# A windowed-attention decoder on one core: scores on alternating row halves, one sine product, VectorE's step reordered

## What is computed

```python
for i in range(DEPTH):                       # 6
    x = attn_layer(shift_tokens(x), Wqkv[i], q_scale[i], k_scale[i], Wo[i]) + x
    x = ffn_layer(shift_tokens(x), ln_g[i], ln_b[i], W1[i], b1[i], W2[i], b2[i]) + x

def attn_layer(x, Wqkv, qs, ksc, Wo):
    q, k, v = (sh(t) for t in jnp.split(x @ Wqkv, 3, -1))      # 16 heads of 64
    q, k = l2norm(q) * qs, l2norm(k) * ksc
    q = q * cos * scale + rotate_half(q) * sin * scale
    k = k * cos * inv + rotate_half(k) * sin * inv
    sim = q @ k.T * QK_SCALE                                   # a key is seen 0 to 32 tokens back
    return softmax(where(mask, -max, sim)) @ v @ Wo            # heads merged before Wo
```

## Time and profile before

| | |
|---|---|
| median of 3 runs | 4648.19 us (4643.84 to 4649.11) |
| the profiled execution | 4650.33 us, span 4648.5 us |
| TensorE matmul / VectorE / ScalarE / GpSimd busy | 93% / 83% / 78% / 73% of the span |
| mean granted clock of TensorE | 0.969 |
| a layer, from one L1460 of VectorE to the next | 658.6 us, of it 542.7 us from the first to the last L1352 (128 of them) |

### The profile page before, as it was taken

One profiled execution on the slowest core, in us unless ns is written; L12 is line 12 of the kernel. 1 busy time (PEld: TensorE's weight loads), 2 busy tenths in 40 slices (PEclk: granted clock), 3 DMA queues, 4 the chain that ended last, 5 costly groups with the idle time before them and its releaser, 6 DMA issues.

```text
span 4648.5 us, 135499 instructions
## 1 busy us (share of the span) xinstructions
PE 4341.6 (93%) x47296; PEld 3494.1 (75%) x47296; DVE 3854.4 (83%) x9773; ACT 3635.1 (78%) x11591; POOL 3383.3 (73%) x2447
## 2 busy tenths in 40 slices
PE   7988869999889999889999799998899998899997
PEld 5666647888768888678888678887688886788886
DVE  7988878888778888778888688887788887788886
ACT  6889967888748888658888478887488886588884
POOL 4544448888658888568888388886588885688882
PEclk9999989999989999989999999999899999899998
DMA  2000000000000000000000000000000000000000
GB/s 76 0 0 1 0 14 2 0 0 0 6 20 1 0 0 0 6 20 0 0 0 1 24 2 0 0 0 6 19 1 0 0 0 6 6 0 0 0 1 19
DMA packets 31380, 26.63 MB, mean 6 GB/s; under 512 B 10308, under 2 KB 23490, under 8 KB 31170
## 3 DMA queue, kind: packets, MB, share of 16 engines
q1 hardware_dynamic: 31170, 23.96, 1.8%
HBM read 21.85 MB, written 2.10 MB: 5 GB/s over the span
## 4 chain that ended last, share of the span: by engine, by line
PE 75%; DVE 12%; issue 7%; ACT 3%; POOL 2%; DVEq 0%; SPq 0%; DMA 0%; ACTq 0%; POOLq 0%
PE bank L659 17%; PE bank L706 13%; PE bank L754 10%; PE bank L732 9%; PE bank L652 7%; PE bank L717 7%; PE bank L820 4%; PE bank L692 4%; DVE top L1270 3%; PE bank L834 2%; DVE qk_parts L1245 2%; PE bank L635 1%; DVE qk_t L1406 1%; DVE by_sin L1238 1%; ACT prob L888 1%
## 5 line engine op out<-in xcount | busy, mean ns | idle before, releaser
L1070 POOL TENSOR_TENSOR rotated<-by_cos,by_sin 128x512 f32<-128x512 f32 x768 | 981.4, 1278 | 394.6 <-DVE by_sin L1320 377.3
L1078 POOL TENSOR_TENSOR rnorm<-norm2g,neg_half 128x16 f32<-128x16 f32 x384 | 1115.5, 2905 | 163.7 <-DVE norm2g L1333 163.7
L963 ACT ACTIVATE bank<-bank,top 128x128 f32<-128x128 f32 x3072 | 1064.1, 352 | 10.9 <-DVE top L1340 4.0
L1090 POOL TENSOR_TENSOR rotated<-rotated,rnorm 128x512 f32<-128x512 f32 x768 | 786.5, 1047 | 0.5
L1312 DVE TENSOR_TENSOR by_cos<-bank,rot_cos 128x512 f32<-128x512 f32 x768 | 531.2, 692 | 256.9 <-PE bank L659 248.6
L945 ACT ACTIVATE qk_t<-bank 128x512 f32<-128x512 f32 x768 | 459.9, 599 | 286.5 <-PE bank L652 285.9
L706 PEld LDWEIGHTS bank<-qk_t 64*64 64x64 f32 x12288 | 529.2, 133 | 193.0 <-issue 193.0
L706 PE MATMUL bank<-qk_t 64*64 64x64 f32 (+1 forms) x12288 | 674.2, 237 | 0.0
L963 ACT ACTIVATION_READ_ACCUMULATOR bank<-bank,top 128x1 f32 x3072 | 669.4, 218 | 0.0
L659 PE MATMUL bank<-wqkv_high,xt_high 128*128 128x512 f32 (+1 forms) x1536 | 598.6, 390 | 11.0 <-ACT vout L974 11.0
L1320 DVE TENSOR_TENSOR by_sin<-bank,rot_sin 128x256 f32<-128x256 f32 x1536 | 572.9, 415 | 0.0
(11 more groups left out here) (148 smaller groups left out, 8904.1 us busy)
## 6 DMA issues: line engine op xcount, KB each, us to landing
wqkv_sb<-in_L_ffn_Wqkv_dram SPq DMA_DIRECT2D x36, 256.0 KB, 4.1
wo_sb<-in_L_ffn_Wo_dram SPq DMA_DIRECT2D x48, 64.0 KB, 2.0
out_dram<-y SPq DMA_DIRECT2D x8, 256.0 KB, 3.5
w_sb<-in_L_ffn_W_dram SPq DMA_DIRECT2D x6, 341.0 KB, 3.0
w_sb<-in_L_ffn_W_dram SPq DMA_DIRECT2D x12, 64.0 KB
cst<-in_constants_dram SPq DMA_DIRECT2D x1, 518.0 KB, 3.5
b_sb<-in_L_ffn_b_dram SPq DMA_DIRECT2D x1, 384.0 KB
w_sb<-in_L_ffn_W_dram SPq DMA_DIRECT2D x6, 42.5 KB
```

The costliest lines, as they stand in the source:

```text
L963: last = nc.scalar.activation(at, at, ACT.Exp, bias=top[jl % 2][:, h:h + 1], accum_out=psum_raw[jl % 2][:, h:h + 1])
L1070: nc.gpsimd.tensor_tensor(rotated[j % 4][:, :, :, :], by_cos[j % 2][:, :, :, :], by_sin[j % 2][:, :, :, :], ALU.add).then_inc(c_rot, 1)
L1078: nc.gpsimd.tensor_tensor(rnorm[slot][:, :, :].rearrange("t g n -> t (g n)"), norm2g[slot][:, :, :].rearrange("t g n -> t (g n)"), neg_hal ...
L1090: nc.gpsimd.tensor_tensor(at, at, rnorm[slot][:, i, :].unsqueeze(2).to_broadcast([P, 2 * HG, DH]), ALU.mult).then_inc(c_unit, 1)
```

## The change

1. **Scores.** A group of four heads is now whole in one step: its heads in rows 0 to 63 (e = 0) write one bank and those in rows 64 to 127 (e = 1) another, and the products alternate between the row halves, and within them between the column halves. A pair of banks (`win_ps`) holds one group's scores, in 256 columns of each; pair45 and pair12 alternate. The mask is bf16 and goes in as four products on the same four quarters of the array.
2. **Banks.** bank1 and bank2 are taken by that, so the projection has bank0 alone (win_project waits for the squares of the group before, c_sq), and turned heads and turned probabilities share bank3 (two new waits between them, c_pt and c_qk).
3. **Sine.** The sine table of the current layer is repeated for the four heads of q and of k (`sin_now`, set by GpSimd in `set_sines` in the MLP stage before the layer), and by_sin is one instruction.
4. **Order.** On TensorE win_heads moves from behind win_turn_next to behind win_scores. On ScalarE win_copy_heads moves to behind win_square. On VectorE the reciprocal is split from the division, and the clamp against the tiny number (`win_clamp`) stands behind win_max; win_tok_next comes after both.
5. wo_sb's rows are ordered by head within the group, since probabilities and values now are.

```diff
@@ -240,10 +240,16 @@
-        bank = [stack.enter_context(nc.psum_tensor(f"bank{i}", [P, 512], F32)) for i in range(8)]
-        proj_ps = bank[0:2]
...
+        bank0, pair12, bank3, pair45, bank6, bank7 = ps("bank0"), ps("pair12", 2), ps("bank3"), ps("pair45", 2), ps("bank6"), ps("bank7")
+        bank = [bank0, pair12[:, 0:512], pair12[:, 512:1024], bank3, pair45[:, 0:512], pair45[:, 512:1024], bank6, bank7]
+
+        win_ps = [t[:, :].rearrange("q (e n) -> q e n", e=2)[:, :, 0:2 * P] for t in (pair45, pair12)]
+        proj_ps = bank[0]
         misc_ps = bank[2]
-        turn_c_ps = bank[2]
+        turn_c_ps = bank[3]
@@ -645,7 +652,9 @@
-                    if has(it * STEPS + j - WIN.turn - 1):
+                    if has(it * STEPS + j - 1 - WIN.probs):
+                        pe.wait_ge(c_pt, g + WIN.turn - WIN.probs)
+                    elif has(it * STEPS + j - WIN.turn - 1):
                         pe.wait_ge(c_qk, g)
@@ -666,11 +675,11 @@
-                    if has(it * STEPS + j - 2):
-
-                        pe.wait_ge(c_sq, g - 1)
+                    if has(it * STEPS + j - 1):
+
+                        pe.wait_ge(c_sq, g)
@@ -678,40 +687,38 @@
+                    for half in range(2):
+                        for e in range(2):
+                            rows, lower = slice(e * DH, (e + 1) * DH), half * DH
+                            nc.tensor.matmul(win_ps[(j - WIN.scores) % 2][lower:lower + DH, e, :].rearrange("q (i k) -> q i k", i=2),
+                                             ident_b[rows, rows], band_b[rows, half, :].unsqueeze(1).to_broadcast([DH, 2, P]),
+                                             start=True, stop=False, skip_group_check=True, tile_position=(e * DH, lower))
...
+                    for i in range(2):
                         for lower, keys in ((0, slice(0, DH)), (DH, slice(WINDOW, P))):
...
+                            for e in range(2):
+                                rows, q0, k0 = slice(e * DH, (e + 1) * DH), i * P + lower, (2 + i) * P
+                                last = nc.tensor.matmul(win_ps[jl % 2][lower:lower + DH, e, i * P + keys.start:i * P + keys.stop],
+                                                        qk_t[jl % 4][rows, q0:q0 + DH], qk_t[jl % 4][rows, k0 + keys.start:k0 + keys.stop],
+                                                        start=False, stop=False, skip_group_check=True, tile_position=(e * DH, lower))
                     last.then_inc(c_scores, 1)
 
             def win_turn_probs(layer, it, j):
                 if here(it, j, WIN.probs):
                     m = layer * GROUPS + it * STEPS + j - WIN.probs
                     jl = (j - WIN.probs) % STEPS
+                    if here(it, j, WIN.turn):
+                        pe.wait_ge(c_qk, layer * GROUPS + it * STEPS + j - WIN.turn + 1)
@@ -765,10 +771,10 @@
                 win_values(layer, it, j)
                 win_mask(layer, it, j)
                 win_scores(layer, it, j)
+                win_heads(layer, it, j)
                 win_sum_values(layer, it, j)
                 win_project_out(layer, it, j)
                 win_turn_next(layer, it, j)
-                win_heads(layer, it, j)
                 win_turn_probs(layer, it, j)
@@ -982,9 +988,9 @@
                 win_square(layer, it, j)
+                win_copy_heads(layer, it, j)
                 win_copy_values(layer, it, j)
                 win_copy_next(layer, it, j)
-                win_copy_heads(layer, it, j)
                 win_copy_probs(layer, it, j)
@@ -1308,17 +1324,16 @@
             def win_sin(layer, it, j):
                 if here(it, j, 0):
...
-                    for a in range(2):
-                        last = nc.vector.tensor_tensor(by_sin[j % 2][:, a, :, :].rearrange("t h (s d) -> t h s d", s=2), got[:, a], sines[:, a], ALU.mult)
-                    last.then_inc(c_sin, 1)
...
+                    rows = lambda b: b[:, :, :, :].rearrange("t a h (s d) -> t (a h) s d", s=2)
+                    nc.vector.tensor_tensor(rows(by_sin[j % 2]), got, rows(sin_now), ALU.mult).then_inc(c_sin, 1)
@@ -1361,10 +1387,12 @@
                 win_cos(layer, it, j)
                 win_sin(layer, it, j)
+                win_recip(layer, it, j)
                 win_scale(layer, it, j)
                 win_norms(layer, it, j)
+                win_max(layer, it, j)
+                win_clamp(layer, it, j)
                 win_tok_next(layer, it, j)
-                win_max(layer, it, j)
                 win_split_next(layer, it, j)
                 win_add(layer, it, j)
```

More of the change, by code:

```diff
@@ L130, in constants @@
     put("causal", np.where(ahead >= 0, 0.0, MASKED))
-    put("band", np.where((ahead >= 0) & (ahead <= WINDOW), 0.0, MASKED))
+    band = np.where((ahead >= 0) & (ahead <= WINDOW), 0.0, MASKED)
+    put("band", np.concatenate([np.tile(band[lower:lower + DH], (2, 1)) for lower in (0, DH)], 1))
     return t
@@ L680, in win_values @@
                         pe.wait_ge(c_vout, layer * VOUTS + it * STEPS + j)
+                    if isinstance(it, int) and 0 <= it * STEPS + j - WIN.scores < 2:
+                        pe.wait_ge(c_qk, layer * GROUPS + it * STEPS + j - WIN.scores + 1)
                     gc = (j % NG) * HG * DH
@@ L685, in win_mask @@
                 if here(it, j, WIN.scores):
-                    m = layer * GROUPS + it * STEPS + j - WIN.scores
-                    if (j - WIN.scores) % 2 == 0:
-                        pe.wait_ge(c_qk, m + 2)
-                    if has(it * STEPS + j - WIN.scores - 2):
-                        pe.wait_ge(c_scaled, m - 1)
-                    nc.tensor.matmul(score_ps[(j - WIN.scores) % 2][:, :].rearrange("q (h k) -> q h k", h=HG), ident_r[:, :],
-                                     band_r[:, :].unsqueeze(1).to_broadcast([P, HG, P]), start=True, stop=False,
-                                     skip_group_check=True)
+                    for half in range(2):
+                        for e in range(2):
[3 more added lines that the diff above has]
+                                             start=True, stop=False, skip_group_check=True, tile_position=(e * DH, lower))
@@ L727, in win_sum_values @@
                     pe.wait_ge(c_pt, m + 1)
-                    e = jl % 2
                     for half in range(2):
-                        for jj in range(HG):
-                            at = 2 * P + (2 * (jj % 2) + e) * DH + half * PAD
-                            last = nc.tensor.matmul(value_ps[PAD * jj:PAD * (jj + 1), half * P:(half + 1) * P],
-                                                    vout[jl - e + jj // 2][:, at:at + PAD], prob_t[jl % 2][:, jj, :],
-                                                    start=True, stop=True, tile_position=(0, PAD * jj))
+                        for h in range(HG):
+                            at = 2 * P + h * DH + half * PAD
+                            last = nc.tensor.matmul(value_ps[PAD * h:PAD * (h + 1), half * P:(half + 1) * P],
+                                                    vout[jl][:, at:at + PAD], prob_t[jl % 2][:, h % 2 * 2 + h // 2, :],
+                                                    start=True, stop=True, tile_position=(0, PAD * h))
                     last.then_inc(c_value, 1)
@@ L953, in win_square @@
                         act.wait_ge(c_nrm2, g)
[L954 removed]
+                    nc.scalar.activation(squares[:, :, :].rearrange("t h d -> t (h d)"), proj_ps[:, :], ACT.Square).then_inc(c_sq, 1)
             def win_exponentials(layer, it, j):
@@ L1117, in mlp_step @@
                         pool.wait_ge(c_vproj, (layer + 1) * GROUPS)
+                        pool.wait_ge(c_sin, (layer + 1) * GROUPS)
+                        set_sines(layer + 1)
                     if not isinstance(it, int) or it * 2 + j - 2 < CHUNKS:
@@ L1148, in _ @@
             pool.wait_ge(s_table_in, 16 * 11)
+            set_sines(0)
             with pool.Fori(0, DEPTH - 1) as layer:
@@ L1328, in win_norms, with win_clamp @@
                     nc.vector.tensor_reduce(pair[:, :, 0:1], squares[:, :, :], AX_X, ALU.add).then_inc(c_nrm2, 1)
+            def win_clamp(layer, it, j):
+                if here(it, j, 0):
+                    g = layer * GROUPS + it * STEPS + j
+                    pair = norm2[j % 2]
                     dve.wait_ge(c_nrm2, g + 1)
```

74 lines of the change are left out of this document (36 added, 38 removed).

## The result

The change takes 4485.27 us, the median of 4 runs (4483.84 to 4488.07), against 4648.65 (4643.84 to 4649.27) for the kernel before beside it: a ratio of 0.9651, 95% interval 0.9639 to 0.9663, 163 us less. The forecast was 4446, with a range of 4375 to 4590. The profiled execution took 4488.07 us, its span is 4486.2, and the mean granted clock is 0.97 as before.

The account below looks back on a forecast made before the run. TensorE's issue bounds the kernel before; after, a chain of waits at 3.88 us a plain step. Four steps fall 1.14 us, 186 times: 4650-212+10 = 4448, less 2 to the median: 4446, range 4375 to 4590.

Parts of the forecast that it names:

- the likeliest case: Whole kernel: the forecast itself, four mid-layer steps 1.14 us shorter, time 4405 to 4500, chance 0.50.
- Rival 3: Scores on TensorE: row halves don't overlap, each step 0.10 us longer, 4734 us, slower; chance 0.10.
- the chain: Plain steps: projection, by_cos, by_sin, squares, copy of heads, probabilities, next projection sum to 3.88 us, over TensorE's 3.82.
- TensorE's own issue: TensorE's instructions alone: 3.82 us in a plain step, 3.89 in the fourth, 4.28 in the input step.
- the saving of 0.36: TensorE's scores and mask: 0.46 us less from overlap, 0.11 back for one more tiling switch, net 0.36 a step.
- Rival 1: Neither the chain nor heads' wait costs anything, TensorE's issue is all: four steps 15.81 us, 4392 us; chance 0.15.
- rival 2: The chain is longer, squares behind exponentials behind prob_t: plain steps 4.10, heads' wait gone, 4535 us; chance 0.20.
- heads' wait, input step 4.46: Input step: heads wait 0.18 us for GpSimd's result, 9.76 against a deadline of 9.58, making the step 4.46.
- the edges: Layer starts: 0.5 us more for each of three steps, 1.6 a layer, 10 us in all, ends 3 and 15.
- The one-bank loop of 3.01: First steps of a layer: projection to next projection with one bank, 3.01 us at full clock against by_cos every 2.84.

Follow-up runs that it names:

- e1: The change with the eight score products of a step ordered row half by row half instead of alternating: 4492.49 us.
- e8: e2 with heads ahead of the mask on TensorE, between values and mask: 4412.25 us.
- e9: e8 with ScalarE's copy of heads ahead of the squares: 4403.34 us.
- e3: The change with by_sin as two products of 256 elements again, on the same repeated table: 4501.74 us.
- e10: e9 with VectorE's maximum ahead of the norms: 4381.81 us.
- e6: e2 with the two waits before the turned probabilities swapped, c_scaled ahead of c_qk: 4453.88 us.
- e2: The change with GpSimd's win_unit ahead of win_rotate in its step: 4433.36 us.
- e5: The kernel before with only by_sin as one product on the repeated table and the clamp behind the maximum: 4649.59 us against 4649.79.
- e4: The change with VectorE's clamp ahead of the maximum again, right behind the norms: 4455.62 us.

## Why the prediction was right, and where it was off

**Right.** Faster by over 0.2% was given 0.85, and the time lies in the likeliest case's own 4405 to 4500. Most of what was named as proof is there: 16 score passes from first to last start in 0.26 us (named: 0.25 to 0.3), starts together across row halves, heads waiting for GpSimd, by_sin at 681 ns with 768 instructions, mid-layer clock 1.00. Two signs are not: eight mid-layer steps take 32.62 and not 32.2, and the profile has TensorE busy in all 3.85 us of a plain step, so no idle time before the probabilities is seen. Rival 3, no overlap of the row halves, was wrong, and e1 shows that the overlap doesn't even need the order. The Trainium skill, TensorEngine Tiling (Array Packing), Key Properties, states that different tiles work in parallel; the four starts within 10 ns agree. The Trainium skill's floor of some 25 ns from start to start (TensorE: Matmul & The Clock Gate, Part 1) is not what these rows show between passes of different tiles: 16 of them start within 0.26, where by that floor the prediction estimated at least 0.40.

**Right, by e8, e9 and e3: the chain.** Plain steps were forecast at 3.88 and are 3.85 and 3.93, 3.89 in the mean. That the mean comes so close is in part luck, since half of them have 0.07 that the sum didn't know. TensorE's own issue, forecast at 3.82, is 3.85 in the change (the mask to heads took 0.57 as summed, but from heads to values it is 0.58, where the saving of 0.36 assumed 0.54), so in the change TensorE and the chain are level and the profile alone could not tell them apart. The three experiments do: 0.15 taken from TensorE's issue (e8) leaves the step, 0.07 put on by_sin (e3) appears in it whole, and with the chain opened half of the plain steps fall to 3.74 to 3.77 (e9), and once e9's loop is out too all are 3.74 to 3.82 (e10). The 0.07 between the two kinds of step is the separate wait of e6, which was not foreseen. Rival 1, TensorE's issue alone and 4392, fell with the heads' wait and those levels; rival 2, plain steps of 4.10, with their 3.89.

**Off: the term "heads' wait, input step 4.46".** It is 4.66 and 4.61, 4.63 in the mean, 0.17 too little, in two parts. The wait itself was put at 0.18 and is 0.29 and 0.24. It was the difference of two long sums, 9.76 for GpSimd's result and 9.58 for its deadline, and the trace shows which was off. GpSimd, between the projection of 2104.77 and the heads of 2114.55:

```profile
2109.33 2.91 POOL L1084 TENSOR_TENSOR rnorm<-norm2g,neg_half 128x16 f32<-128x16 f32 x1 [0.93 <-DVE norm2g L1353]
2112.20 1.29 POOL L1076 TENSOR_TENSOR rotated<-by_cos,by_sin 128x512 f32<-128x512 f32 x1
2113.44 2.06 POOL L1096 TENSOR_TENSOR rotated<-rotated,rnorm 128x512 f32<-128x512 f32 x2
```

The result came 9.78 behind that projection, as summed. The deadline was early, 2x3.85+1.79 = 9.49, by the two steps of 0.03 and the 0.03 of heads' place. In the other kind of four the sums are 9.88 and 9.64. And TensorE's own input step was put at 4.28; e2, without the wait, shows 4.37. There were split wrongly: a window of 4.64 was read as the input step, and the 4.25 left over as a fourth kind of step, while in the trace before there are three of 4.18 and 4.19 and one of 4.70. With the same sum and 4.70 the own input step would have been 4.34.

So a mid-layer four saves 0.95 and not 1.14: over 31 fours and six layers 177 us and not 212, which is 35 of the 40 us missed by the profiled execution (4488 against 4448). The terms of the prediction's chain as printed add up to 3.87 and those of GpSimd's path to 9.77; this 0.01 changes nothing.

**Off: the edges, by 5.** The first three steps of a layer take 10.97 where they took 8.68: 3.66 each, 0.76 more, where 0.5 had been taken. The one-bank loop of 3.01 at full clock is stretched by 0.65. Busy time in these steps, after, as in the earlier trace rows:

```profile
1957.00:1969.40 12.40, 8.15 (x23) 6.12 (x23) 6.92 (x15) 2.62 (x6) 6.95 (x5) 0.50 0.02 9
```

The granted clock is 0.50 there, the lower of its two levels, and the 0.64 that the prediction read in the earlier trace rows was the mean of a longer window. From the projection's start to by_cos it is 1.68 (1960.39 to 1962.07), where 0.98 was taken at full clock, and TensorE's next projection is released by ScalarE's squares, so the loop is the one that was named. With what lies between two layers five of the six lose 2.9 each, and not 1.6, and the last 2.0; the time ahead of the first layer is 2.0 shorter. Together that is 15 us, where 10 had been taken.

**Costed at nothing, rightly:** VectorE's shorter step by itself (e5). **Not seen as a cost:** the clamp behind the maximum. The prediction said that it makes GpSimd's result late, and booked the wait, but not that this edit alone had caused it: e4 gives 30 us back.

## What to carry to other kernels

When two engines' resources are swapped (here banks of PSUM for overlap on TensorE), write out the chain that the fewer buffers close, and test it by shortening the engine that the profile calls busy: if the step stays, something else binds, and lengthening one link of the chain (here by_sin) shows whether it is the chain. A step repeated 768 times must be split from starts, not by subtracting windows, and each edit's effect on the slowest consumer (here GpSimd's deadline at heads) should be summed for that edit alone. The best order here came from asking at each stall who is last: GpSimd's unit first, heads before the mask, the copy before the squares, the maximum before the norms, together 103 us.

## What the runs showed of the hardware

- Four tiles of 64x64, two row halves by two column halves, run f32 passes together when each row half writes a bank of its own: 16 passes from first to last start in 0.26 us, for the 0.63 of the earlier trace rows on one row half. With one bank for both row halves it wasn't tried.
- Passes of a tile whose turn in the program is later start ahead of waiting passes of other tiles: by the records within 19 ns of the first, with eight in front (e1).
- Of two waits ahead of a weight load, the one that comes last costs 0.07 us more where it stands as an instruction of its own than where the load carries it (e6, and the two kinds of four).
- A change of tiling between 64x64 and 128x128, booked at 0.11 with the first weights, costs some 0.15 in this place, first weights included: with one of them less, e8's values start 2.23 into the step and not 2.38.
